# Moving ScalarE's hat functions, norm roots and one weight product inside a convolution, state-space and routing kernel

## The reference, cut to what matters

```python
x = x + deformable_conv(group_norm(x))              # 3x3 taps, offsets and masks from a first convolution
t = tokens(x)
t = t + mamba_both_ways(layer_norm(t))              # 8 sequences of 256 tokens, forward and backward
t = t + experts_with_graph_gate(layer_norm(t), edges)
```

```python
cols = sum(gather(y, x) * wy * wx for the 4 corners) * 2 * sigmoid(mask)
out  = cols @ kernel + bias
xn   = (x - mean) / sqrt(var + 1e-5)
```

## Time and profile before

| what | value |
|---|---|
| median of 3 runs | 747.19 us (746.07 to 747.66) |
| the profiled execution | 746.95 us, its span 745.2 us |
| PE, DVE, ACT, POOL busy | 74%, 82%, 40%, 39% of the span |
| instructions | 11002 |
| TensorE's mean granted clock | 0.821 of full |

### The profile page before, as it was taken

How to read it: one execution, slowest core, us unless ns; L and a number is a source line. 1 busy time by engine, 2 the same in 40 slices (tenths; PEclk the granted TensorE clock), 3 DMA queues, 4 the chain that set the end, 5 groups by cost and what they waited for, 6 DMA issues and landing times.

```text
span 745.2 us, 11002 instructions
## 1 busy us (share of the span) xinstructions
PE 551.7 (74%) x4083; PEld 354.4 (48%) x4083; DVE 610.3 (82%) x1196; ACT 297.4 (40%) x343; POOL 288.4 (39%) x179
## 2 busy tenths in 40 slices
PE   3578898989999986965688887798797777970040
PEld 2168787878888983421232332232233274750030
DVE  4999948576798969767899999899999727379987
ACT  2431313223123115487778555465555403320040
POOL 4033303020220200034566576566666603777304
PEclk9889796969999995987699999899999965555555
DMA  8300000000000001000000000000000000011100
GB/s 217 76 1 3 0 4 1 3 8 2 3 2 9 3 8 40 1 0 0 0 0 0 0 0 0 1 0 0 0 0 0 0 1 13 10 9 7 4 2 28
DMA packets 17585, 8.46 MB, mean 11 GB/s; under 512 B 14691, under 2 KB 16771, under 8 KB 17283
## 3 DMA queue, kind: packets, MB, share of 16 engines
q1 hardware_dynamic: 15746, 7.26, 3.7%
q0 software_dynamic: 1792, 0.58, 1.6%
HBM read 6.58 MB, written 1.25 MB: 11 GB/s over the span
## 4 chain that ended last, share of the span: by engine, by line
PE 41%; DVE 32%; issue 16%; ACT 8%; DMA 1%; DVEq 1%; POOL 0%; ACTq 0%; SPq 0%; POOLq 0%
PE ps L579 10%; PE ps L587 9%; DVE ps L1297 9%; PE ps L606 3%; PE ps L794 3%; PE ps L563 3%; DVE arena L1304 3%; PE ps L714 2%; PE ps L806 2%; PE ps L757 2%; DVE arena L1484 2%; DVE g L1486 2%; ACT arena L866 1%; PE ps L667 1%; DVE arena L1156 1%
## 5 line engine op out<-in xcount | busy, mean ns | idle before, releaser
L478 POOL TENSOR_TENSOR arena<-arena 128x1024 f32<-128x1024 f32 x64 | 150.6, 2355 | 83.9 <-DVE arena L1304 32.7
L1304 DVE TENSOR_TENSOR_SCAN arena<-arena,ps 128x1024 f32<-128x1024 f32 x64 | 146.3, 2287 | 10.3 <-ACT arena L951 2.1
L714 PE MATMUL ps<-arena,ident 128*128 128x512 f32 x256 | 128.1, 629 | 30.2 <-POOL arena L478 30.2
L450 POOL TENSOR_TENSOR arena<-arena 128x1280 f32<-128x1280 f32 x16 | 39.6, 2497 | 191.3 <-DVE arena L1171 164.7
L955 ACT ACTIVATE arena<-ps 128x1024 f32<-128x1024 f32 x64 | 65.5, 1023 | 75.6 <-POOL arena L478 55.5
L714 PEld LDWEIGHTS ps<-arena,ident 128*128 128x128 f32 x256 | 46.8, 197 | 94.2 <-POOL arena L478 54.2
L1297 DVE TENSOR_TENSOR ps<-arena,ps 128x1024 f32<-128x1024 f32 x64 | 77.3, 1208 | 2.3 <-PE ps L700 2.2
L579 PE MATMUL ps<-arena 128*128 128x64 f32 x576 | 78.8, 304 | 0.0
L951 ACT ACTIVATE arena<-arena,neg_a 128x1020 f32<-128x1020 f32 x64 | 73.2, 1144 | 9.8 <-DVE arena L1291 4.2
L579 PEld LDWEIGHTS ps<-arena 128*128 128x128 f32 x576 | 76.5, 218 | 1.2
L866 ACT ACTIVATE arena<-ps 128x768 f32<-128x768 f32 x48 | 37.3, 809 | 93.7 <-PE ps L606 93.7
(11 more groups left out here) (313 smaller groups left out, 751.0 us busy)
## 6 DMA issues: line engine op xcount, KB each, us to landing
arena<-dram_edges SPq DMA_DIRECT2D x2, 1024.0 KB, 7.5
arena<-dram_x SPq DMA_DIRECT2D x2, 512.0 KB, 5.3
arena<-node_rows,src_idx POOLq DMA_INDIRECT x56, 2.6
x_tok<-dram_x SPq DMA_DIRECT2D x1, 512.0 KB, 10.3
res_scratch<-x_tok SPq DMA_DIRECT2D x4, 128.0 KB, 2.0
arena<-res_scratch SPq DMA_DIRECT2D x1, 512.0 KB, 3.2
w<-dram_w SPq DMA_DIRECT2D x3, 128.0 KB, 2.6
out<-arena SPq DMA_DIRECT2D x1, 352.0 KB, 2.2
```

The costliest lines, as they stand in the source:

```text
L478: g.tensor_tensor(gg[e], hh[e], cs[e], ALU.mult).then_inc(s["g_ready"], 1)
L714: m = pe.matmul(ps[:, 4 + q, :], ident[:], gg[e][:, 512 * q:512 * q + 512], start=False, stop=True, skip_group_check=True)
L1304: v.tensor_tensor_scan(o, x0, x1, 0.0, ALU.mult, ALU.add).then_inc(s["scan_ready"], 1)
```

## The change

Three moves, with no arithmetic added or taken away. In ScalarE's tile loop the hats go from tiles 2, 4, 6 to tiles 3, 5, 7, and hats and roots come to stand between the two xk copies of their tile. Behind the loop, part 0 of the xn2 copies goes ahead of root 6. On TensorE the two dt weight products go ahead of the wait for `xnt_ready`.

```diff
@@ tensor
                 if i in (NT - TPQ - 1, NT - 1):
                     m.then_inc(s["xnt_psum"], 1)
+            pe.wait_ge(s["base_read"], 1)
+            pe.wait_ge(s["wmamba_in"], 2 * 8 * 16)
+            for d in range(2):
+                pe.matmul(ps[:, 7, DI * d:DI * d + DI], xd_w[d][:], dp_w[d][:], start=True, stop=True).then_inc(s["dtw_psum"], 1)
             pe.wait_ge(s["xnt_ready"], 4)
             pe.wait_ge(s["taps_ready"], 4)
-            pe.wait_ge(s["wmamba_in"], 2 * 8 * 16)
-
-            pe.wait_ge(s["base_read"], 1)
-            for d in range(2):
-                pe.matmul(ps[:, 7, DI * d:DI * d + DI], xd_w[d][:], dp_w[d][:], start=True, stop=True).then_inc(s["dtw_psum"], 1)
@@ scalar
                 if i < NT - 2:
                     xk_copy(4 + 2 * i)
-                    xk_copy(5 + 2 * i)
-                if i in (2, 4, 6):
+                if i in (3, 5, 7):
                     hats(i // 2)
-
                 if i >= 6 and i % 2 == 0:
                     ln_root(i // 2 - 3)
+                if i < NT - 2:
+                    xk_copy(5 + 2 * i)
             ln_root(5)
-            ln_root(6)
             act.wait_ge(s["s_ready"], NT)
             act.wait_ge(s["s2_ready"], NT)
             for part in range(2):
@@ scalar
                 f(xn2[:, sl, 1, :], x_tok[:, sl], ACT.Copy).then_inc(s["xn2_ready"], 1)
                 if part == 0:
+                    ln_root(6)
                     ln_root(7)
```

## The result

The changed kernel takes 726.83 us in the median of 4 runs (725.23 to 727.9), the kernel before 746.63 (745.09 to 747.66, 4 runs). The ratio is 0.9735, 95% interval 0.9706 to 0.9764: faster by 2.65%. The profiled execution took 725.86 us (span 724.0) where that of before took 746.95, a difference of 21.1 us.

A forecast was written before the change was run, and what follows sets the result against it. It took TensorE's chain to be held up by ScalarE's hats, paid as idle time and then half clock. From 746.95 us, -22.5 + 0.1 + 1.3 = -21.1 gave 725.9, range 722.9 to 731.5.

The forecast's parts named there:

- The hats out of the even tiles, 22.52: Tiles 2 to 7: without hats the three two-tile stretches become like clean ones of 27.69 us, saving 22.52 us.
- The rival that only the stall would go: Tiles 3, 5, 7: the clock falls all the same, gain only 9.7 us, time 737.3; chance 0.09.
- The split into stall (9.7) and half clock (12.8): Tiles 3, 5, 7: of the 22.5 us gain, half clock was 3 x 4.28 = 12.8, leaving 9.7.
- The hats in odd tiles, 0: Tiles 3, 5, 7: about 2.6 us of hats fit into ScalarE's 4.77 us idle time; cost 0.
- VectorE's new wait: At masks(1) VectorE waits about 1.4 us for the later hats, leaving 1.3 us of slack; cost 0.
- become the bound: Tile loop rival: VectorE's wait for hats exceeds its slack, some 2 us, time 728; chance 0.04.
- Roots and loads between the copies, 0.1: Even tiles 6 to 14: roots fit between the xk copies; table loads in tiles 6 and 8 cost 0.1 us.
- One fall of the clock put back, 1.3: Even tiles: one clock fall like tile 6's is added back, 1.3 us; ends 0 and 3.9.
- The rival on the slower side: Tiles 2 to 7: all six conv tails at half clock, 25.7 us lost, net +3.2, time 750.2; chance 0.02.
- Behind the loop, 0: After the tile loop: moving the xn2 copies and dt product earlier gains 0, as VectorE releases the payload product (L682).
- the cost that I named and took as 0: Ahead of the payload product: longer idle time lets the clock fall, 1.3 to 2.9 us; as a rival, chance 0.15.
- The upper end with its terms: Whole kernel: high end 731.5 us, from three clock falls, table loads at 0.4 and 1.3 to 2.9 behind the loop.

The follow-up runs named there:

- the fillers: The kernel before, with unused identity products on TensorE in its idle time in tiles 3, 5 and 7; 738.1 us, ratio 0.9865.
- The third buffer: The changed kernel with a third buffer for tap products, so an even tile's first xk copy needn't wait for the conv tail; 722.99 us, ratio 0.967.
- second profiled execution of the changed kernel: The changed kernel, unaltered, run again beside one with only its tile loop changes; median 727.41 us, ratio 0.9728, profiled 725.86 us.

## Why the prediction was right

The forecast was 725.9 us out of the profiled execution of 746.95; the profiled execution of the changed kernel took 725.86, the median is 726.83.

- **The hats out of the even tiles, 22.52.** The three stretches gave 34.67 + 35.10 + 35.82 - 27.70 - 27.69 - 27.69 = 22.51. That both were to be had is shown: the tails of tiles 3, 5 and 7 took 4.16 us, and they did so with the fillers in the idle time too. The rival that only the stall would go falls with it. The split into stall (9.7) and half clock (12.8) was off, though. TensorE idled 2.34, 2.33 and 2.57 us ahead of the third transposes where 0.30 is usual, 6.3 us too much in all. The rest, some 16 us, was half clock, which had begun ahead of the tails. The sum did not need the split; the price of that rival did.
- **The hats in odd tiles, 0.** Right: they end 2.18 us before ScalarE is wanted in tile 3, and 0.77 in tile 7, with the table load.
- **VectorE's new wait.** 1.4 us forecast, 1.36 measured; slack 1.3 forecast, 1.19 measured. What I named as late next was wrong: with the hats later still, TensorE first waited for the conv sums behind masks(1), not for one-hots. VectorE did not become the bound.
- **Roots and loads between the copies, 0.1.** The stretch of tile 6 has 27.69, so 0. The rule of the Trainium skill ("ScalarE: Activation LUTs", What ACT_TABLE_LOAD costs) that each table switch costs a drain of some 1.38 us besides the load is not what this trace shows: the load starts at 131.83, 0.02 us behind the copy ahead of it, and the root 1.29 us later, at 133.12. The two loads that the change adds are in tiles 7 and 8, not 6 and 8 as I wrote there. What I had missed is how much this place is worth. With the loads exposed they cost 5.4 us, 3.5 of it by a clock fall. I had put the whole 22.52 down to the hats and taken the roots' move as a part that changes nothing, but without it the third stretch doesn't become clean.
- **One fall of the clock put back, 1.3.** There was one, in tile 8, for 28.84 - 27.69 = 1.15 us. The third buffer showed that the 0.56 us wait is needed for it: without it there was no such fall in the profiles of the four kernels that have the buffer, six such tiles in each, while each of the six profiles with two buffers and the hats in odd tiles has just one, in tile 4, 8 or 12. I had put back just one on the strength of a single trace, and that it held was in part luck. The rival on the slower side, in which all six tiles fall, had this mechanism but not its frequency: one tile in the first profile and one in the second.
- **Behind the loop, 0.** This is the term that was mis-sized. The gain of 0 was right, but the cost that I named and took as 0, the clock falling ahead of the payload product, came in five of seven profiles with the dt product moved. The payload product then took 1.6 us more, inside the 1.3 to 2.9 that I gave, and the whole 1.0 to 2.1 us, by the means and ratios above. The idle time ahead of it, which I put at 2.1 or 2.7 us, was 3.43: the projection started 1.13 us earlier against the payload product, as reckoned, but it also took 9.20 us and not 9.91. The profiled execution is one of the two in seven in which the payload product was fast, so that its 725.86 meets the forecast to the tenth is luck; the median of 726.83 is the fairer measure. Whether slow payload products make the median 0.97 higher stays open, since the unprofiled runs have no trace. Their granted clocks are 0.842 and 0.837 at 727.9 and 727.8 us, against 0.851 and 0.848 at 725.86 and 725.23, but the second profiled execution of the changed kernel had 0.848 and 725.86 us with a slow one.
- **Small slips in the sums.** The upper end with its terms (0.4, 3.9 and 2.9) gives 731.65, not 731.5. Where VectorE was reckoned, 17.7 less 14.2 is 3.5 us, not 3.4. The payload product started 21.34 us earlier, not about 22. None of these moves the forecast.

## What to carry to other kernels

Where TensorE waits for another engine, look at the granted clock behind the wait before pricing it: here three idle times of 2.33 to 2.57 us cost 22.5 in all, some 16 of it as half speed afterwards. Work that an in-order engine does for later tiles belongs where that engine is waiting already, here in the tile whose first copy meets a free buffer, beside a conv tail; a table load counts as such work. Starting a small product earlier when the next large one is held by someone else saved nothing here, and it left a longer idle time ahead of the large one, in front of which the clock fell in five of seven profiles.

## What the runs showed of the hardware that was not expected

- The same stall of about 1.1 us ahead of a conv tail (idle times of 1.39 and 1.43) was followed by a tail of 7.25 us in one tile and of 4.16 two tiles later, in one execution. Idle times of 2.46 us brought the clock down ahead of one payload product, 3.43 and 3.54 us did not ahead of others.
- Right behind a wait of 0.56 us TensorE fell to half clock in tile 8, and in other executions in tile 4 or 12. With that wait removed it kept 1.00 from tile 2 to the end of the loop, in four profiles.
- A table load took 1.28 us in every place. Beside a wait of ScalarE's it cost 0; on the path it cost 0.95 us in one tile and, with the fall of the clock behind it, 4.45 in another.
- Products that nobody reads, put into three idle times of TensorE, made the kernel before 9.1 us faster (738.1 against 747.18).
